# Score stage: chunk 1 of each tile seeded too, the rests written over the raw pieces, and 24 instead of 16 of 36 pieces rounded on GpSimd

## The reference, cut to what matters

```python
def _lap_mul(A, x):                                   # A, x: (8192, 8192), (8192, 128), float32
    d = 1.0 / jnp.sqrt(jnp.sum(A, axis=-1))
    return d[:, None] * (A @ (d[:, None] * x))
z = leaky_relu(_lap_mul(A, x) @ W1 + b1, 0.1)
sq = jnp.sum(z * z, axis=-1)
d2 = jnp.maximum(sq[:, None] + sq[None, :] - 2.0 * (z @ z.T), 0.0)
S = jnp.exp(-jnp.sqrt(d2 + 1e-10) / 2.0)
S = S where it is among the 4 largest of its row, else 0
out = _lap_mul(S + A, x) @ W2 + b2
return layernorm(x + out)
```

## Time and profile before

| what | value |
|---|---|
| time, median of 3 runs | 2680.91 us (2680.7 to 2683.14) |
| the profiled execution's own time | 2679.84 us |
| its span, first to last instruction | 2678.0 us |
| busy PE, DVE, ACT, POOL (share of the span) | 92%, 87%, 60%, 45% |
| score stage, first tile search to the last one's end | 1048 to 2259 us |
| matmuls of line 880 (square terms) | 280 |
| seeds on ACT (line 1133) | 372 |
| roundings on ACT (line 1118), on POOL (line 1300) | 152, 112 |
| rests on POOL (line 1305) | 264, 2439 ns each |

### The profile page before, as it was taken

The page is one execution under the profiler, slowest core; times in us unless marked ns, Lnnn a source line. Parts: engine busy times, 40 slices in busy tenths (PEclk is TensorE's granted clock), DMA queues, the critical chain, the costliest instruction groups (busy, mean ns, idle before and its releaser), DMA issues.

```text
span 2678.0 us, 29073 instructions
## 1 busy us (share of the span) xinstructions
PE 2456.8 (92%) x9356; PEld 1710.4 (64%) x9356; DVE 2319.3 (87%) x1411; ACT 1606.8 (60%) x1905; POOL 1193.2 (45%) x987
## 2 busy tenths in 40 slices
PE   0467999999999999899999999999999998899998
PEld 0133444444577777577778787877878775577776
DVE  7998889976788887999999999989999877488887
ACT  0000000000377776899998989889898876477776
POOL 0000000000000000067788888878787895777772
PEclk9678999999999999999999999999999999999999
DMA  9999999997699981035565555545555568999996
GB/s 383 421 405 402 399 421 421 421 421 291 236 374 345 341 329 52 0 114 170 147 170 147 168 149 141 175 135 177 146 173 148 168 179 320 398 400 402 400 402 244
DMA packets 147948, 718.58 MB, mean 268 GB/s; under 512 B 19024, under 2 KB 26960, under 8 KB 86608
## 3 DMA queue, kind: packets, MB, share of 16 engines
q1 hardware_dynamic: 124384, 670.49, 66.7%
q0 software_dynamic: 18800, 37.77, 5.7%
q10 hardware_dynamic: 4608, 8.39, 0.8%
HBM read 680.40 MB, written 36.18 MB: 268 GB/s over the span
## 4 chain that ended last, share of the span: by engine, by line
PE 59%; DMA 9%; issue 9%; DVE 9%; ACT 9%; POOL 3%; SPq 0%; ACTq 0%; POOLq 0%; DVEq 0%
PE PS L773 19%; PE PS L872 5%; PE PS L874 5%; PE PS L873 5%; DMA ring<-at 4%; ACT R L1147 3%; PE PS L840 3%; DMA R<-at 3%; PE PS L916 3%; PE PS L917 3%; PE PS L927 3%; PE PS L836 2%; PE PS L837 2%; PE PS L977 2%; DVE R L1629 2%
## 5 line engine op out<-in xcount | busy, mean ns | idle before, releaser
L1305 POOL TENSOR_TENSOR al<-ring,ah 128x1024 fp32r<-128x1024 f32 x264 | 643.7, 2439 | 181.6 <-ACT ah L1118 168.0
L1629 DVE MAX8 R<-R 128x8 f32<-128x8192 f32 x64 | 555.8, 8685 | 68.6 <-ACT R L1147 68.4
L1147 ACT ACTIVATE R<-PS 128x1024 f32<-128x1024 f32 x512 | 518.0, 1018 | 112.0 <-PE PS L880 82.6
L1632 DVE FIND_INDEX8 R<-R,R 128x8 uint32<-128x8192 f32 x64 | 555.9, 8685 | 0.3 <-issue 0.3
L1278 POOL CAST zst<-zh 128x128 fp32r<-128x128 f32 (+1 forms) x64 | 26.3, 411 | 1112.8 <-DVE zl L1564 811.1
L872 PE MATMUL PS<-zh,zst 128*128 128x512 f32 x1024 | 407.2, 398 | 28.5 <-ACT PS L1133 12.7
L874 PE MATMUL PS<-zh,zst 128*128 128x512 f32 x1024 | 400.4, 391 | 0.0
L873 PE MATMUL PS<-zl,zst 128*128 128x512 f32 x1024 | 400.2, 391 | 0.0
L1133 ACT ACTIVATE PS<-R 128x1024 f32<-128x1024 f32 x310 | 318.0, 1026 | 6.6
L1052 ACT ACTIVATE tiny<-rowsum 128x4 f32<-128x4 f32 x16 | 3.3, 205 | 482.1 <-DVE rowsum L1499 482.1
L773 PE MATMUL PS<-cache,R 128*128 128x512 f32 x584 | 263.5, 603 | 16.7 <-DMA cache<-at 11.3
(11 more groups left out here) (181 smaller groups left out, 4515.5 us busy)
## 6 DMA issues: line engine op xcount, KB each, us to landing
R<-at SPq DMA_DIRECT2D x160, 1024.0 KB, 14.7
ring<-at SPq DMA_DIRECT2D x148, 1024.0 KB, 9.4
ring<-at SPq DMA_DIRECT2D x264, 512.0 KB, 3.8
cache<-at SPq DMA_DIRECT2D x117, 1024.0 KB, 20.3
acc_dram<-R POOLq DMA_DIRECT2D x78, 256.0 KB, 5.7
raw_sq<-at SPq DMA_DIRECT2D x18, 1024.0 KB, 14.4
raw_z<-at SPq DMA_DIRECT2D x18, 1024.0 KB, 15.3
raw_ring<-at SPq DMA_DIRECT2D x17, 1024.0 KB
```

The lines of the kernel that those rows point to most:

```text
L1147: act.activation(score[j % 2][:, c * EC:(c + 1) * EC].rearrange("p (b c) -> p b c", b=2), pair(first, j, c), ACT.Copy).then_inc(copied, 1)
L1305: pool.tensor_tensor(al[:, k % SPLIT], raw[k % RAW], ah[:, k % SPLIT].bitcast(F32), ALU.subtract)\
L1629: v.max(top[:, j], score[j % 2]).then_inc(dve3, 1)
L1632: v.max_index(place[:, j], top[:, j], score[j % 2]).then_inc(placed, 1)
```

## The change

Chunk 1 is seeded as well, so that only chunk 0 stays plain. A seventh stored row is needed (`sq_more`, 4 KB in each partition). Room for it comes from the `al` buffers: the rest is now written over the raw piece itself. There are four raw buffers, two `ah` buffers and no separate `al`. A raw buffer is therefore loaded again only when PE has read the rest in it (`prodb` in place of `rest`), and POOL's own wait for `prodb` goes.

ACT seeds chunk 1 of the next tile right after the copy of chunk 7, ahead of a rounding that stands there. `on_pool` gives POOL the pieces whose number isn't a multiple of 3, 24 of 36 in place of 16; group 0 keeps every third. SP's store of xg with its halves, and its load of the next xg, move back by one piece, since their places count from `RAW`.

```diff
-RAW, SPLIT, BANKS = 3, 2, 2
-SEEDED = (3, 4, 5, 6, 7, 2)
+RAW, SPLIT, BANKS = 4, 2, 2
+SEEDED, SEED_ORDER = (3, 4, 5, 6, 7, 1, 2), (2, 1, 3, 4, 5, 6, 7)
+ROWS_R2 = 5
 PLAIN_TILES = 2
-ON_POOL = tuple(range(1, HB * (GT // 2) - 4, 2))
+ON_POOL = tuple(k for k in range(HB * (GT // 2)) if k % 3)
...
-        al = sb("al", [P, SPLIT, PT, BC], F32R, at=over + SPLIT * PIECE * 4)
-        xgh = sb("xgh", [P, GT, D], F32R, at=over + 2 * SPLIT * PIECE * 4)
+        al = [sb(f"al{i}", [P, PT, BC], F32R, at=top_of["ring"] + i * PIECE * 4) for i in range(RAW)]
+        xgh = sb("xgh", [P, GT, D], F32R, at=over + SPLIT * PIECE * 4)
...
+        sq_more = sb("sq_more", [P, 2, BC], at=over + SPLIT * PIECE * 4 + GT * D * 4)
+        sq_row[SEEDED[-2]] = sq_more[:, :, :]
...
-            return k % RAW == RAW - 1 if is_first(g) else k in ON_POOL
+            return k % 3 == 2 if is_first(g) else k in ON_POOL
...
-                        sp.wait_ge(rest, pieces_before(g) + (k - RAW + 1))
+                        sp.wait_ge(prodb, pieces_before(g) + (k - RAW + 1))
...
-                    pe.wait_ge(seeded, len(SEEDED) * (GT * g + j - PLAIN_TILES) + c - SEEDED[-1] + 1)
+                    pe.wait_ge(seeded, len(SEEDED) * (GT * g + j - PLAIN_TILES) + SEED_ORDER.index(c) + 1)
...
-                            seed(SEEDED[-1])
+                            for k in SEED_ORDER[:2]:
+                                seed(k)
...
+                        last = is_last(g) and j == GT - 1
+                        if c == NE - 1 and not (first and j < PLAIN_TILES) and not last:
+                            act.wait_ge(copied, NE * (GT * g + j) + c + 1)
+                            seed(SEED_ORDER[1])
                         for back, k in pieces_at(g, j, c):
...
-                if not (isinstance(g, int) and n < SPLIT):
-                    pool.wait_ge(prodb, n - SPLIT + 1)
-                    hold(pool)
                 wait_rounded(pool, g, k)
-                pool.tensor_tensor(al[:, k % SPLIT], raw[k % RAW], ah[:, k % SPLIT].bitcast(F32), ALU.subtract)\
+                pool.tensor_tensor(al[k % RAW][:, :, :], raw[k % RAW], ah[:, k % SPLIT].bitcast(F32), ALU.subtract)\
```

More of the change, by code:

```diff
@@ L241, in build @@
         ah = sb("ah", [P, SPLIT, PT, BC], F32R, at=over)
-        al = sb("al", [P, SPLIT, PT, BC], F32R, at=over + SPLIT * PIECE * 4)
-        xgh = sb("xgh", [P, GT, D], F32R, at=over + 2 * SPLIT * PIECE * 4)
+        al = [sb(f"al{i}", [P, PT, BC], F32R, at=top_of["ring"] + i * PIECE * 4) for i in range(RAW)]
+        xgh = sb("xgh", [P, GT, D], F32R, at=over + SPLIT * PIECE * 4)
         acc = R2[:, 0:HB * BC]
-        sq_row = {c: R2[:, i * EC:(i + 1) * EC].rearrange("p (b c) -> p b c", b=2) for i, c in enumerate(SEEDED[:-1])}
+        sq_row = {c: R2[:, i * EC:(i + 1) * EC].rearrange("p (b c) -> p b c", b=2) for i, c in enumerate(SEEDED[:ROWS_R2])}
         over_sq = sb("over_sq", [P, 2, 2, BC], at=top_of["sqn"])
         sq_row[SEEDED[-1]] = over_sq[:, :, 1]
-        at_ = [max(HB * BC, (len(SEEDED) - 1) * EC)]
+        sq_more = sb("sq_more", [P, 2, BC], at=over + SPLIT * PIECE * 4 + GT * D * 4)
+        sq_row[SEEDED[-2]] = sq_more[:, :, :]
+        at_ = [max(HB * BC, ROWS_R2 * EC)]
         def cut(n):
@@ L923, in second_half @@
                 xgh_g = halves_of(odd)[0]
-                (ib, p), u, s = at_piece(g, k), unit(g, k), k % SPLIT
+                (ib, p), u = at_piece(g, k), unit(g, k)
                 pe.wait_ge(rest, pieces_before(g) + k + 1)
                 for kk in range(PT):
-                    i = pe.matmul(bank_of(g, odd, u), xgh_g[:, p * PT + kk], al[:, s, kk], start=False,
+                    i = pe.matmul(bank_of(g, odd, u), xgh_g[:, p * PT + kk], al[k % RAW][:, kk], start=False,
                                   stop=closes(g, k) and kk == PT - 1)
@@ L1171, in group_act @@
                                 round_piece(*following(g - back, k))
-                        if c + 3 in SEEDED and not (first and j < PLAIN_TILES):
+                        if c + 3 in SEED_ORDER and not (first and j < PLAIN_TILES):
                             act.wait_ge(copied, NE * (GT * g + j) + c + 1)
                             seed(c + 3)
-                        last = is_last(g) and j == GT - 1
-                        if c == SEEDED[-1] + 3 and not (first and j < PLAIN_TILES) and not last:
+                        if c == SEED_ORDER[0] + 3 and not (first and j < PLAIN_TILES) and not last:
                             act.wait_ge(copied, NE * (GT * g + j) + c + 1)
-                            seed(SEEDED[-1])
+                            seed(SEED_ORDER[0])
                         for back, k in pieces_at(g, j, c):
```

## The result

The changed kernel took 2686.32 us (median of 14 runs), the kernel before it 2681.8 (14 runs beside them). The ratio is 1.0018, with a 95% interval from 1.001 to 1.0025. The forecast was 2689 with a range of 2677 to 2698. So the sign is right, and the size is somewhat over half: 4.5 us where the forecast stood 8.1 above the median that it started from (2680.91). The 4.5 us lie inside the 5.4 us that were taken as the limit of what can be told from no change: by that bound the outcome is the "within 0.2%", to which the forecast gave 0.25, and not the "slower" of 0.62. The interval of these runs is narrower than that bound and leaves 1 outside. The profiled execution of the changed kernel took 2684.8, its span is 2683.0; 2678.0 was the span before.

The account below looks back on a forecast made before the run. Bounds differ by stretch: ACT and DVE early, PE's matmul rate in free runs, POOL's chain, POOL in the last group. 2.0 + 7.6 - 15.0 + 6.8 + 7.2 = +8.6 on 2679.84 gave 2688.4; forecast median 2689, range 2677 to 2698.

Parts of the forecast that it names:

- three signs of being wrong: Early stretch keeps its length; PE doesn't wait for POOL in tile 2; PE waits at chunk 1 in the free run.
- Start: First tiles: the seventh stored row's matmuls wait for ACT to copy the fifth row, +2.0 us (bounds 1.1 and 3).
- Early stretch: Tiles 7 to 18: twelve added seeds of 1.10 us on ACT, which has little idle time, +7.6 us (6.5 to 11).
- Free runs: Five, piece 2 to piece 30 (next group's tile 1): fewer PE matmuls, -3.0 us each, together -15 (-19 to -8).
- rival of the late seed: Free runs: PE waits for chunk 1's seed, losing the 2.74 us saved in each; sum +8.6 + 13.7, 2703 us; chance 0.08.
- Chain stretches: Four, piece 30 to next piece 2: POOL's added roundings make PE wait, +1.7 us each, together +6.8 (-5 to +12).
- Last group: Final five tiles, POOL-bound: enters 1.7 us late, eight more roundings cost 8.9, 3.4 regained from idle; +7.2 (3.8 to 10).
- What follows the score stage: Work after the scores: waits for their end and moves with it, its DMAs keeping their own length; no change forecast.
- The blocked search: Rival: POOL's added casts block DVE's index search, 8.9 us more per 148.8 us cycle; 2697 us; chance 0.02.
- The mechanisms: Main forecast 0.70; POOL's chain has cover and ACT's relief decides (2675 us) 0.20; late seed 0.08; blocked search 0.02.

## Why the prediction was right, point by point

**The balance.** The argument was that the free runs' saving is real, and that what ACT and POOL get in exchange at the start, in the early stretch, in tile 2 and in the last group eats it. The ledger has each of these with the sign given, and none of the three signs of being wrong came: the early stretch grew, PE waits for POOL in tile 2, and it doesn't wait at chunk 1 in the free run. The sizes are off by 1 to 3 us each: the losses behind the start were put too high, the loss at the start too low and the gain of the free runs too high.

**Start, +2.0 forecast, +3.81 measured** (bound 3). This is the one term above its bound. The step reckoned ACT's idle time and one copy. It left out that PE stands still meanwhile, and what its clock does then. PE begins tile 2's scores at 1071.79 where it was 1069.40, 2.39 later; the other 1.42 come behind that, in chunk 0. TensorE in the changed kernel, from the sixth row, then the one matmul and the window of before:

```profile
1068.43 2.08 PE L897 MATMUL PS<-sqn,sel 128*128 128x512 f32 x4 [2.03 <-ACT R L1132]
1071.79 0.77 PE L875 MATMUL PS<-zh,zst 128*128 128x512 f32 x1 [1.28 <-issue]
1072.36 0.63 PE L876 MATMUL PS<-zl,zst 128*128 128x512 f32 x1
...
1075.36 0.40 PE L876 MATMUL PS<-zl,zst 128*128 128x512 f32 x1
```
```profile
1069.40 0.47 PE L872 MATMUL PS<-zh,zst 128*128 128x512 f32 x1 [2.06 <-issue]
1068.00:1075.20 7.20, 5.80 (x26) 4.83 (x27) 7.05 (x3) 5.89 (x7) 0.00 (x0) 1.00 0.00 0
```

After waits of 2.03 and 1.28 us the matmuls take 0.63 in place of 0.40, one every 0.43 in place of 0.23, until 1075. The granted clock in these 7.2 us is 0.53: the lower of the two levels, 1.2 in place of 2.4 GHz. In the kernel before the same window had 1.00, with 26 matmuls where there are 13 now. In the version with the other order of rows, where the first wait is 1.11, the clock stayed at 1.00 and the term was +0.97.

**Early stretch, +7.6 forecast, +6.14 measured** (bounds 6.5 and 11, so a little below the lower). That ACT is the bound and has no room was right; its groups, which answer, and the same twelve tiles of before:

```profile
L1150 ACT ACTIVATE R<-PS 128x1024 f32<-128x1024 f32 x96 | 96.3, 1015 | 0.3 <-DVE R L1636 0.3
...
L1136 ACT ACTIVATE PS<-sq_more 128x1024 f32<-128x1024 f32 x12 | 12.3, 1029 | 0.4
```
```profile
1155.76:1372.19 216.43, 208.99 (x898) 166.72 (x898) 208.73 (x39) 209.66 (x232) 162.50 (x144) 1.00 0.52 151
```

The waits before copies went from 5.5 to 0.3. ACT's busy time grew by 10.24 for exactly twelve more instructions, and its idle time shrank by 4.67: 5.57 in all, and the last 0.57 come between tile 18's search and piece 2. So a seed added about 0.85 and not 1.10: the mis-sized term. The price of 1.10 came from three instructions back to back; a queue that never has to wait overlaps more of its neighbours, which would fit, but no run separates that. The row that shows the bound from the other side is the version with group 0's roundings on POOL: ACT 208.0 of 214.5, and the stretch is shorter than before.

**Free runs, -15 forecast, -13.6 measured.** Four of five gave 2.95 in the mean (2.67 to 3.29), as reckoned (-3.0): 482 x 0.2285 = 110.1, and the row has 110.16. PE hardly waited for a seed from the first free run to the end of the stage (total us, times, longest):

```profile
PE PS L875 <- ACT PS L1136: 0.7, 3, 0.3
```

So the rival of the late seed is out. The fifth free run gave 1.83, since PE's pause at the loop's turn was 1.25 longer (last section).

**Chain stretches, +6.8 forecast, +3.91 measured.** The order of events is as described. GpSimd and TensorE in the changed kernel, through the same tiles as the earlier trace rows:

```profile
1518.15 2.15 POOL L1374 TENSOR_TENSOR R<-R,tiny 128x1024 f32<-128x1024 f32 x1
1519.99 1.27 POOL L1307 CAST ah<-ring 128x1024 fp32r<-128x1024 f32 x1
...
1524.66 1.03 POOL L1307 CAST ah<-ring 128x1024 fp32r<-128x1024 f32 x1
```
```profile
1521.32 0.50 PE L919 MATMUL PS<-ah,xgh_odd 128*128 128x512 f32 x1 [2.37 <-POOL ah L1307]
...
1522.65 0.63 PE L875 MATMUL PS<-zh,zst 128*128 128x512 f32 x1
...
1534.76 0.50 PE L919 MATMUL PS<-ah,xgh 128*128 128x512 f32 x1
...
1539.16 0.50 PE L919 MATMUL PS<-ah,xgh 128*128 128x512 f32 x1
```

PE waits for POOL's rounding of piece 34, behind `scale_xg`. From PE's piece 30 (1495.32 before, 1502.16 after) to piece 34 it is 18.02 before and 19.16 after, to piece 1 again 13.42 and 13.44, to piece 2 4.20 and 4.40: +1.14, +0.02, +0.20. I had +1.5, +0.24 and about zero. Two steps were mis-sized. `scale_xg` starts 15.99 after piece 30 and not 17.04, so it is 1.05 ahead and not 0.48. And the wait of 2.37 is longer than 1.5 because PE itself arrives 1.23 earlier; after it the clock falls again (matmuls of 0.63 from 1522.65, granted clock 0.50 for 3.4 us), which doesn't show as further lateness at piece 1, where PE used to wait 0.60; the roundings alone gave equal stretches with and without that fall. The first and third chain stretch grew by 1.36 and 1.34, the second and fourth by 0.57 and 0.64; why they alternate wasn't tried. That POOL is the cause is shown from both sides: the roundings alone bring the loss, and two roundings fewer take it away.

**Last group, +7.2 forecast, +5.92 measured.** POOL without idle time, as said; its groups, which answer:

```profile
L1309 POOL TENSOR_TENSOR al<-ring,ah 128x1024 fp32r<-128x1024 f32 x34 | 82.3, 2430 | 1.9
L1307 POOL CAST ah<-ring 128x1024 fp32r<-128x1024 f32 x23 | 26.4, 1146 | 0.0
```

Of the 7.2, 1.7 were POOL's lateness at entry and 5.5 the work behind it. The rests of the group's first and last piece, before and after:

```profile
2121.11 2.66 POOL L1305 TENSOR_TENSOR al<-ring,ah 128x1024 fp32r<-128x1024 f32 x1
...
2235.71 2.37 POOL L1305 TENSOR_TENSOR al<-ring,ah 128x1024 fp32r<-128x1024 f32 x1 [0.39 <-ACT ah L1118]
```
```profile
2122.80 2.42 POOL L1309 TENSOR_TENSOR al<-ring,ah 128x1024 fp32r<-128x1024 f32 x1
...
2241.82 2.37 POOL L1309 TENSOR_TENSOR al<-ring,ah 128x1024 fp32r<-128x1024 f32 x1
```

PE's piece 30 of (7,1) starts at 2094.33 and 2094.55. So POOL's first rest comes 26.78 behind it before and 28.25 after: 1.47 late, near the 1.7. From the first rest to the last it is 114.60 and 119.02, +4.42 where 5.5 was put down: POOL's idle time shrank by 3.3, as taken (3.4), but its busy time grew by 7.7 and not by 8.9, as the rests came out shorter (2473 and 2430 ns in the mean there).

**What follows the score stage** was 1.2 shorter. Over the ten executions it is between 434.3 and 440.0 in kernels that don't touch it, so this is its own scatter.

**The blocked search.** The Trainium skill ("SBUF — State Buffer", section "Who interferes with whom") says that a VectorE instruction with two SBUF inputs contends with a GpSimd instruction that reads SBUF. The index search takes 8685 ns in the mean before and after, with 48 more casts on POOL: this trace shows no such contention for it, and the rival is out.

**The chances.** The mechanisms were put at 0.70, 0.20, 0.08, 0.02, and the first is what happened. But four terms came out lower than reckoned (early -1.5, chain -2.9, last -1.3, behind the stage -1.2) and two higher (start +1.8, free runs +1.4): the sum went from +8.6 to +5.0. Taken without sign the misses add up to 10 us; that the total is off by 3.6 alone is partly luck. So is the third free run: behind the same pause the half clock would have made it 2.8 longer (last section). A likeliest value so close to the bound of 0.2% should have put about as much on "within" as on "slower".

## What to carry to other kernels

Work that is moved to a helper engine is worth its price only where the engine that gives it away is late: here the removed matmuls carried 2.2 of the 2.95 us that a free run gained, and relief for ACT alone brought 0.6. In the chain stretch the best of the three shares tried is the one where the busy times of the two engines lie closest (with 16, 24 and 22 roundings on POOL: ACT 35.6 and POOL 31.9, then 31.8 and 34.4, then 33.8 and 32.9 us, and the stretch 36.6, 36.5 to 37.0, and 34.7). A share that is set by one rule for all groups loses in the stretches that are bound in another way; setting it for each stretch, with the other order of rows, turned a loss of 0.2% into a gain of 0.7%. And a wait that one adds to TensorE may have to be priced with its clock: at the start one of 2.03 us made +3.81 of a reckoned +2.0, while in the chain stretches the fall of the clock cost nothing that can be seen.

## What the runs showed of the hardware

**TensorE's clock falls after short waits, but not always.** At the start the wait was 2.06 us in the kernel before, and the granted clock stayed at 1.00; with the buffers alone changed, at the same place and after the same wait of 2.06, it was this:

```profile
1069.20:1076.00 6.80, 6.19 (x15) 4.86 (x16) 6.65 (x3) 3.59 (x4) 0.00 (x0) 0.50 0.00 0
```

That made the start 2.6 us longer (39.86 in place of 37.23) with the same instructions. So part of the +3.81 may come and go between executions. But all five executions with the changed kernel's order of rows had 0.50 there for at least 6.8 us, both with the other order had 1.00, and so had the roundings alone. What decides it isn't told by these runs.

**The loop's turn costs TensorE a pause of its own, and the clock can nearly double it.** Groups 1 to 6 run in a loop, and in the third free run PE comes to its first scores behind the turn after a pause in which it waits for nothing that the profile shows. In the kernel before, in the changed kernel, in the one with the last group's roundings as before, and in the one with group 0's on POOL:

```profile
1764.12 0.49 PE L872 MATMUL PS<-zh,zst 128*128 128x512 f32 x1 [1.86 <-issue]
```
```profile
1769.37 0.49 PE L875 MATMUL PS<-zh,zst 128*128 128x512 f32 x1 [3.11 <-issue]
1769.70 0.40 PE L876 MATMUL PS<-zl,zst 128*128 128x512 f32 x1
```
```profile
1770.14 0.79 PE L877 MATMUL PS<-zh,zst 128*128 128x512 f32 x1 [3.11 <-issue]
1770.72 0.63 PE L878 MATMUL PS<-zl,zst 128*128 128x512 f32 x1
```
```profile
1763.99 0.79 PE L875 MATMUL PS<-zh,zst 128*128 128x512 f32 x1 [4.37 <-issue]
1764.58 0.63 PE L876 MATMUL PS<-zl,zst 128*128 128x512 f32 x1
```

The second and third run the same code here and pause for the same 3.11 us. Behind it the matmuls take 0.40 in the one and 0.63 in the other, and the free run 114.29 and 117.05. Where the pause is 4.37, the run takes 118.21: this is where part of the gain of group 0's edit went. The pause is 1.6 to 1.9 before and with the buffers alone, and between 3.0 and 4.6 in all others; why is open. Of these eight two kept the clock at 1.00 behind it (the changed kernel and the one with the other order of rows: free runs of 114.29 and 114.21), and six did not (116.94 to 118.49).
